# Node update of a two-layer graph network: the engines' order of work over five batches instead of three

## The reference

```python
# layer 0, after the edges have been summed into agg (12500 x 64)
out = ssp(agg @ w_o1 + b_o1) @ w_o2 + b_o2        # ssp(v) = softplus(v) - log 2
x = layernorm(x + out)                            # 12500 x 128
# layer 1, before its edges
xw = x @ W
dinv = rsqrt(deg)
# messages of layer 1: xw[src] * dinv[src] * dinv[dst]
```

## Time and profile before

| | us |
|---|---|
| median of 3 runs | 9237.99 (9237.7 to 9241.23) |
| the profiled execution | 9238.26 |
| its span | 9236.5 |
| busy: PE, DVE, ACT, POOL | 5857.3, 5990.5, 2841.2, 7009.1 |
| mean granted TensorE clock | 0.731 of 2.4 GHz |

### The profile page before, as it was taken

One profiled execution on the slowest core, in us unless ns is written; L12 is line 12 of the kernel. 1 busy time (PEld: TensorE's weight loads), 2 busy tenths in 40 slices (PEclk: granted clock), 3 DMA queues, 4 the chain that ended last, 5 costly groups with the idle time before them and its releaser, 6 DMA issues. The chain is left out here.

```text
span 9236.5 us, 170683 instructions
## 1 busy us (share of the span) xinstructions
PE 5857.3 (63%) x45794; PEld 3977.4 (43%) x45794; DVE 5990.5 (65%) x18699; ACT 2841.2 (31%) x4623; POOL 7009.1 (76%) x5303
## 2 busy tenths in 40 slices
PE   5656555655665565566556565545477787777775
PEld 3434444434444443444444344433355555555552
DVE  2777777777777777777777777763455555555554
ACT  2333333333333333333333333323322222222224
POOL 2788888888888888888888888883477777777771
PEclk5666666666666666666666666665599999999996
DMA  4333333333333333333333333332422222222222
GB/s 155 30 30 31 31 30 31 30 31 30 31 30 31 31 30 31 30 31 30 31 30 31 31 30 31 30 28 85 132 75 76 76 76 76 76 76 77 76 75 75
DMA packets 785265, 462.11 MB, mean 50 GB/s; under 512 B 621864, under 2 KB 735252, under 8 KB 784474
## 3 DMA queue, kind: packets, MB, share of 16 engines
q0 software_dynamic: 556608, 301.40, 28.5%
q1 hardware_dynamic: 219372, 145.20, 5.6%
q10 hardware_dynamic: 9246, 15.06, 0.5%
HBM read 301.15 MB, written 160.10 MB: 50 GB/s over the span
## 5 line engine op out<-in xcount | busy, mean ns | idle before, releaser
L1029 POOL DMA_INDIRECT agg_tab<-big x3224 | 5000.3, 1551 | 1002.7 <-issue 910.1
L1504 POOL DMA_INDIRECT big<-y_parts,big x1856 | 1811.5, 976 | 612.5 <-issue 603.7
L883 DVE TENSOR_SCALAR_CACHE_REDUCE big<-ps,big 128x512 bf16<-128x512 f32 x806 | 2006.5, 2489 | 111.9 <-PE ps L752 70.4
L752 PE MATMUL ps<-big 2*128 2x512 bf16 x806 | 471.6, 585 | 2395.1 <-DVE big L883 2395.1
L752 PEld LDWEIGHTS ps<-big 2*128 2x128 bf16 x806 | 78.8, 98 | 2603.9 <-DVE big L883 2603.2
L1588 ACT CAST big<-ps 128x980 bf16<-128x980 f32 x684 | 667.0, 975 | 1678.9 <-PE ps L1534 1677.9
L928 DVE TENSOR_SCALAR big<-big,trash 128x8 uint32<-128x8 f32 x403 | 93.5, 232 | 1532.0 <-DMA agg_tab<-big 1531.1
L1546 PE MATMUL ps<-big 128*128 128x384 bf16 x5586 | 1041.5, 330 | 0.0
L914 DVE SCALAR_TENSOR_TENSOR big<-ps,srcF,big 128x128 bf16<-128x128 f32 x3224 | 931.8, 344 | 0.0
L1640 DVE TENSOR_SCALAR big<-big,dstF 128x343 bf16<-128x343 f16 (+2 forms) x2736 | 827.6, 334 | 128.4 <-PE ps L1534 121.1
L739 PE MATMUL ps<-big 128*128 128x128 f32 x3224 | 835.4, 441 | 0.0
(11 more groups left out here) (226 smaller groups left out, 9429.7 us busy)
## 6 DMA issues: line engine op xcount, KB each, us to landing
big<-in_edge_attr SPq DMA_DIRECT2D x403, 128.0 KB
agg_tab<-big POOLq DMA_INDIRECT x3224, 3.2
big<-y_parts,big POOLq DMA_INDIRECT x1856
big<-h_parts SPq DMA_DIRECT2D x403, 48.0 KB
agg_tab<-big POOLq DMA_DIRECT2D x12, 1056.0 KB, 7.7
big<-agg_tab SPq DMA_DIRECT2D x100, 125.0 KB
big<-y_parts SPq DMA_DIRECT2D x2, 4704.0 KB, 33.3
y_parts<-big SPq DMA_DIRECT2D x25, 375.0 KB
```

The lines of the kernel that those rows point to most:

```text
L752: pe.matmul(ps_dst, m.split[:, :], drow[s][:, 512 * q:512 * q + 512], start=True, stop=True).then_inc(dst_out, 1)
L883: nc.vector.tensor_scalar(pick[s].rearrange("w (j e) -> w e j", j=J)[:, half * q:half * q + half, :], ps_dst.rearrange("w (e j) -> w e j", ...
L1029: nc.gpsimd.indirect_dma_start(out=m.agg_tab[k][:, :], out_offset=bass.IndirectOffsetOnAxis(ap=sidx[s][:, j:j + 1], axis=0), in_=summed[s] ...
L1504: nc.gpsimd.indirect_dma_start(out=m.grow[t % 2][:, 3 * D * j:3 * D * j + 3 * D], out_offset=None, in_=m.y_parts[:, :], in_offset=bass.Ind ...
```

## The change

The operations, their sizes, the buffers and what each operation waits for are the same; only the wait ahead of a load is written for the later batch. The diff, cut to its core (the bodies of ACT's new small functions are the lines of before, moved):

```diff
+def staged_wide(eng, n, stage):
+    def near(k):
+        return {d: (k + d, (k + d) % 2, (k + d) // 2) if 0 <= k + d < n else None for d in range(-2, 4)}
+    for k in range(-3, 4):
+        stage(near(k))
+    with eng.Fori(0, (n - 7) // 2) as i:
+        for c in (4, 5):
+            stage({d: (2 * i + c + d, (c + d) % 2, i + (c + d) // 2) for d in range(-2, 4)})
+    for k in range(n - 3, n + 2):
+        stage(near(k))
...
             # SP
-            def stage(before, here, after):
-                if here and not (isinstance(here[0], int) and here[0] + 2 >= NB):
-                    g, s, _ = here
-                    sp.wait_ge(agg_sum, ready(g, 2))
-                    load(g + 2, s)
-                if before:
-                    store(*before[:2])
+            def stage(at):
+                if at[3] and not (isinstance(at[3][0], int) and at[3][0] < 2):
+                    g, s, _ = at[3]
+                    sp.wait_ge(agg_sum, ready(g, 0))
+                    load(g, s)
+                if at[-2]:
+                    store_parts(*at[-2][:2])
+                if at[-1]:
+                    store_y(*at[-1][:2])
+                    store_x(*at[-1][:2])
...
             # POOL
+                if at[1]:
+                    sum_tables(*at[1])
+                if at[-2]:
+                    split_y(*at[-2][:2])
...
             # PE
+                if at[1]:
+                    turn_agg(*at[1][:2])
+                if at[-2]:
+                    turn_y(*at[-2][:2])
+                if at[-1]:
+                    turn_x(*at[-1][:2])
+                if at[0]:
+                    output(*at[0][:2])
+                if at[1]:
+                    hidden(at[1][0])
+                if at[-1]:
+                    times_w(at[-1][0])
...
             # ACT
+                if at[1]:
+                    copy_agg(at[1][0])
+                if at[-2]:
+                    mid_part(*at[-2][:2])
+                if at[-1]:
+                    copy_x(at[-1][0])
+                if at[1]:
+                    abs_relu(at[1][0])
+                if at[0]:
+                    norm_root(nc, act, norm, *at[0][:2])
+                if at[-1]:
+                    scale_y(*at[-1])
+                if at[1]:
+                    exp_ln(at[1][0])
+                if at[-1]:
+                    high_part(*at[-1])
...
             # DVE
+                if at[0]:
...
                     dve.wait_ge(x1_stored[s], 16 * turn + 16)
                     dve.sem_inc(norm.waited, 1)
                     dve.wait_ge(x_turned, free(g))
                     dve.sem_inc(norm.waited, 1)
                     norm_rows(nc, dve, m, norm, g, s, xn[s])
+                if at[1]:
+                    g, s, _ = at[1]
+                    dve.wait_ge(ln_made, ready(g, 1))
+                    dve.wait_ge(out_made, free(g))
+                    nc.vector.tensor_tensor(hid[s], relu, log1p, ALU.add).then_inc(hid_done, 1)
+                if at[-1]:
+                    g = at[-1][0]
+                    dve.wait_ge(y_turned, ready(g, 2))
+                    nc.vector.tensor_copy(rows[:, bass.ds(g * B, B), :],
+                                          ps_yT.rearrange("f (t p) -> f t p", t=B)).then_inc(yT_copied, 1)
```

More of the change, by code:

```diff
@@ L1170, in load, with store_x @@
                                  ).then_inc(tabs_in[s], 16)
-            def store(q, s):
+            def store_x(q, s):
                 sp.wait_ge(norm.normed, ready(q, 2))
@@ L1175, in store, with store_y @@
                              xn[s]).then_inc(x1_stored[s], 16)
+            def store_y(q, s):
                 sp.wait_ge(y_scaled, ready(q, 1))
@@ L1178, in store, with store_parts @@
                              yb[s]).then_inc(y_stored[s], 16)
+            def store_parts(q, s):
                 sp.wait_ge(y_low, ready(q, 1))
@@ L1185, in _ @@
             sp.dma_start(m.dinv_tab.rearrange("(p c) -> p c", p=NP), m.dinv[:, :]).then_inc(dinv_stored, 16)
-            def stage(before, here, after):
-                if here and not (isinstance(here[0], int) and here[0] + 2 >= NB):
-                    g, s, _ = here
-                    sp.wait_ge(agg_sum, ready(g, 2))
-                    load(g + 2, s)
-                if before:
-                    store(*before[:2])
-            staged(sp, NB, stage)
+            def stage(at):
[8 more added lines that the diff above has]
+                    store_x(*at[-1][:2])
+            staged_wide(sp, NB, stage)
             sp.wait_ge(y_stored[0], 16 * (NB // 2 + 2))
@@ L1236, in split_y, with stage @@
                 nc.gpsimd.tensor_tensor(yp[s][:, :, 2, :], left, yp[s][:, :, 1, :], ALU.subtract).then_inc(y_low, 1)
[L1238 to L1243, removed]
+            def stage(at):
+                if at[1]:
+                    sum_tables(*at[1])
+                if at[-2]:
+                    split_y(*at[-2][:2])
+            staged_wide(pool, NB, stage)
         @block.tensor
@@ L1294, in turn_y, with stage @@
                 tr.then_inc(y_turned, 1)
[L1296 to L1308, removed]
+            def stage(at):
+                if at[1]:
[10 more added lines that the diff above has]
+                    times_w(at[-1][0])
+            staged_wide(pe, NB, stage)
         @block.scalar
@@ L1323, in _ @@
             act.wait_ge(dinv_steps, 2)
[L1325 to L1367, removed]
@@ L1368, in _, with copy_agg, copy_x @@
-            staged(act, NB, stage)
+            def copy_agg(g):
+                act.wait_ge(agg_turned, ready(g, 2))
+                if not isinstance(g, int) or g:
+                    act.wait_ge(hid_made, g)
+                nc.scalar.copy(aggT, ps_a).then_inc(agg_copied, 1)
+            def copy_x(g):
+                act.wait_ge(x_turned, ready(g, 2))
+                if not isinstance(g, int) or g:
+                    act.wait_ge(y_made, g)
+                nc.scalar.copy(xT, ps_xT).then_inc(xT_copied, 1)
@@ new lines, in abs_relu, with exp_ln @@
+            def abs_relu(g):
+                act.wait_ge(hid_made, ready(g, 0))
+                act.wait_ge(hid_done, free(g))
+                nc.scalar.activation(log1p, ps_h, ACT.Abs, bias=m.bo1_s[:, 0:1]).then_inc(act_steps, 1)
+                nc.scalar.activation(relu, ps_h, ACT.Relu, bias=m.bo1_s[:, 0:1])
+            def exp_ln(g):
+                act.wait_ge(act_steps, 2 * g + 1)
+                nc.scalar.activation(log1p, log1p, ACT.Exp, scale=-1.0).then_inc(act_steps, 1)
+                act.wait_ge(act_steps, 2 * g + 2)
+                nc.scalar.activation(log1p, log1p, ACT.Ln, scale=0.5, bias=m.half[:, 0:1]).then_inc(ln_made, 1)
@@ new lines, in scale_y, with high_part @@
+            def scale_y(g, s, turn):
+                act.wait_ge(y_made, ready(g, 0))
+                act.wait_ge(y_stored[s], 16 * turn + 16)
+                act.wait_ge(y_turned, free(g))
+                for t in range(B):
+                    last = nc.scalar.activation(yb[s][:, D * t:D * t + D], ps_y[:, D * t:D * t + D], ACT.Copy,
+                                                scale=m.dinv[:, bass.ds(g * B + t, 1)])
+                last.then_inc(y_scaled, 1)
+            def high_part(g, s, turn):
+                act.wait_ge(y_scaled, ready(g, 1))
+                act.wait_ge(parts_stored[s], 16 * turn + 16)
+                nc.scalar.copy(yp[s][:, :, 0, :], yb[s].rearrange("p (t d) -> p t d", t=B)).then_inc(y_high, 1)
@@ new lines, in mid_part, with stage @@
+            def mid_part(g, s):
+                act.wait_ge(y_left, ready(g, 0))
+                nc.scalar.copy(yp[s][:, :, 1, :], y_rest.rearrange("p (t d) -> p t d", t=B)).then_inc(y_mid, 1)
+            def stage(at):
+                if at[1]:
[14 more added lines that the diff above has]
+                    high_part(*at[-1])
@@ L1370, in _ @@
+            staged_wide(act, NB, stage)
         @block.vector
@@ L1383, in _, with stage @@
             nc.vector.reciprocal(m.dinv[:, :], m.dinv[:, :]).then_inc(dinv_steps, 1)
-            def stage(before, here, after):
-                if here:
-                    g, s, _ = here
+            def stage(at):
+                if at[0]:
+                    g, s, turn = at[0]
                     dve.wait_ge(x_biased, ready(g, 0))
@@ L1394, in stage @@
                     norm_measure(nc, dve, m, norm, g, s)
[L1395 to L1401, removed]
                     dve.wait_ge(x1_stored[s], 16 * turn + 16)
@@ L1406, in stage @@
                     norm_rows(nc, dve, m, norm, g, s, xn[s])
-                if before:
-                    g = before[0]
+                if at[1]:
[5 more added lines that the diff above has]
+                    g = at[-1][0]
                     dve.wait_ge(y_turned, ready(g, 2))
@@ L1411, in stage @@
                                           ps_yT.rearrange("f (t p) -> f t p", t=B)).then_inc(yT_copied, 1)
-            staged(dve, NB, stage)
+            staged_wide(dve, NB, stage)
 def graph_layer(nc, m, io):
```

## The result

The changed kernel takes 9150.15 us (median; 9146.76 to 9150.53), the kernel before 9239.61 in the same runs: ratio 0.9902, 95% interval 0.989 to 0.9914. That is 89 us, where 55 were forecast; the time stands on the lower edge of the range, and the ratio applied to the 9238.26 us that the prediction started from gives 9147.7, just under it. The profiled execution took 9149.82 us with a span of 9147.8, so 88.7 us of span went. No instruction of the other phases changed: the first transfer behind the node update is issued 91.0 us sooner (6552.05 for 6643.04), and 2.3 us of this are lost again in the last phase.

What follows compares the result with a forecast made beforehand. The kernel was taken as bound by a ring of engine waits, then by DMA: first y_parts issue at 6285, 21 intervals of 12.8 us, then 27, ending 6580.8; 55.5 us saved from 9238.3 gives 9183 us, range 9150 to 9243.

Steps and rivals of the forecast that it cites:

- the ring: Node update before the change: GpSimd, TensorE and ScalarE steps of a batch wait on each other in series, 15.34 us per batch.
- the DMA term: Node update after the change: 1.41 MB a batch through five DMA engines sets the period, 12.8 us, between 11.4 and 14.6.
- half of the gain: y_parts store: 6.4 us at 60 GB/s, 3.1 at 124 in a full queue; half the saving assumed, 12.8 us per batch.
- the count of intervals without loads: End of the node update: the last three y_parts intervals have no loads and take 27 us, after 21 of 12.8.
- The loops: Longest dependency loops between engines in the new order: a batch each 8 to 10 us, 9.5 taken, below the DMA's period.
- side sum for GpSimd: Worst order around mid_part's new wait: all of GpSimd's 5.4 us plus mid_part's 0.6, 6.5 us, covered by 9.5.
- upper bound of 14.6: Node-update period if the DMA keeps its present speeds and only its gaps close: 15.34 x 0.298 / 0.3125 us.
- mid_part's wait: ScalarE's mid_part, now second in its stage, waits for GpSimd's subtraction; worst loop 7.7 us, covered by 9.5.
- DVE's early copy: DVE's copy of turned y might pull batches together again; its loop of 6.5 to 7.4 us and hand-overs counted as covered.
- DMA is no bound: Rival: the DMA ceiling comes from transfer spacing, not engines; 9.5 us a batch, 9113 us; chance 0.07.
- Lost in the queue: Rival: y_parts stays slow and gaps remain as waits pass on delay; 14.6 to 15.5 us, 9220 to 9240; chance 0.14.
- slower: Rival: the five DMA engines run at their slow rates throughout; 16.4 us a batch, 9258 us, or 17 and 9271; chance 0.08.

Runs made afterwards that it cites:

- Sixteen engines: Each node-update transfer cut into 112 and 13 partitions: kernel before 9784.53 us against 9790.69 uncut; changed kernel 9076.38 us against 9239.25 for the kernel before.
- the bytes: Changed kernel with two more loads per batch, 9193.77 us, or two fewer from the third batch on, 9111.84; unaltered changed kernel beside them 9156.06.

## Why the prediction was right and where it was wrong

The mechanism was right: the ring is cut, and five engines' worth of DMA takes over. The step that failed is the size of the DMA term, "I take half of the gain: 12.8 us per batch": it measured 11.45. With it failed the count of intervals without loads in the sum, three where there are five.

*The kernel before is bound by the ring, not by an engine or the DMA*: shown. Sixteen engines change nothing in its rhythm (353.0 for 353.5 us), and under the new order they give 194.3.

*The loops allow 8 to 10 us, 9.5 taken*: the size was a little high. (In its side sum for GpSimd, L1233's end to 6433.49 is 0.86 us, not 0.6; the 6.5 that it gives fits the 0.86.) Freed of the DMA they run at 8.1 to 8.4, with the granted clock at 0.82 to 0.90, where I had kept 0.62 for PE alone.

*The DMA takes over, five engines are the ceiling, 11.4 to 14.6 us*: the mechanism is shown by cutting the transfers and by the bytes. The term was mis-sized within its bounds: I took half of y_parts' gain, 12.8 (half of the 3.3 us over 11.4 would have been 13.0); it is the whole gain, 11.45 in the middle. I had written that the store would stand in a full queue as x and y do at 124 GB/s, and had no reason for the half beyond caution. The upper bound of 14.6 was high as well: with the measured ceiling of 0.33 in place of 5/16 it is 15.34 x 0.298 / 0.33 = 13.9. The mis-sized term is 1.35 x 21 = 28 of the 35.6 us by which the 21 intervals came out shorter (233.2 for 268.8).

*The end of the sum*: two of those 21 intervals are 7.8 and 7.5 us, since loads are issued one batch further ahead and y_parts one stage later; I had counted three intervals without loads, there are five. That is the other 7 us. The last three took 26.5 for 27, and the first issue came at 6284.0 for 6285. What I left unchanged behind the last issue grew: the next phase's first transfer is 8.3 us behind it, not 6.75 as before, and the phase began 0.7 us later. The last issue came 37.1 us sooner than forecast; these 1.6 us and the 2.3 lost in the last phase leave 33.2 of it in the span.

*The range*: the lower end, 9150, stood 3 us under the time for a period of 11.4, with nothing for an error elsewhere in the sum, while the upper reached 60 us up from the forecast. The bound itself held (1.41 MB at 124 GB/s); the two short intervals took the time down to the edge.

*Waits*: norm_rows waits for DMA at its store of x, as named; mid_part's wait was put at nothing and costs 1.1 us a batch beside the DMA, so nothing. DVE's early copy is in no long wait.

*The rivals*: "DMA is no bound" falls. "Lost in the queue" and "slower" fall for the diff as it is; but the queue is where the diff could have lost: with SyncE's old order the time is 69 us over the kernel before. I had counted the x store's move on SyncE and not the load's ahead of y_parts; without SyncE's part of the diff there is no gain.

## What to carry to other kernels

Ahead of a reordering that overlaps more, divide the bytes per round by the best rate that these very transfers have shown, and read the DMA share against its own ceiling, not against 1: tiles of 125 partitions had a ceiling of a third. Where that bound is below the new period, it is the result; a transfer that is slow on an empty queue is to be priced at the full queue's rate if the queue will be full. And the queue's order is part of the schedule: with each load issued behind the store that waits for the end of the round, the period here was 18.8 us, and 11.4 with loads ahead of it.

## What the runs showed of the hardware that I had not expected

The same store of 0.38 MB ran at 58 to 61 GB/s when issued on an empty queue with loads at its heels (the kernel before, and the changed one with SyncE's old order, with quite different work on the engines), at 80 to 84 on an empty queue with only other stores at its heels, and at 130 in a queue with work ahead of it. The share of sixteen engines reached 0.33 to 0.34 where I had computed with 5/16.

In one group of runs the last phase took some 550 us longer for all kernels (before 9790.69, not 9239), and GpSimd's idle time between its gathers there was 1168 us in place of 613, while the node update kept its 353 us. The cause is open; it isn't shown to be the chip, since the record gives the same chip number for a later group with 9244.09.
